# Decoder layer on one core: the first two batches of attention output products issued ahead of the third shifted scores

## The chip, the cores and the metric

The kernel runs on one core of a Trainium2 chip. The metric is the device time of one execution in microseconds; the time of a kernel is the median of several executions. The profile is of one more execution. Its engines are called PE (TensorE matmuls), PEld (TensorE weight loads), DVE (VectorE), ACT (ScalarE), POOL (GpSimd) and SP (SyncE, which here issues DMAs).

## What is computed

A pre-norm decoder layer over x of 128 batches x 128 tokens x 256 features, in float32, 16 heads of 16 features:

```
x = x + self_attention(layernorm(x))
x = x + cross_attention(layernorm(x), ctx, mask)
x = x + ffn(layernorm(x))          # 256 -> 1024 (ternary weights), gelu, layernorm, 1024 -> 256 (ternary weights)

attention: Q, K, V = projections with biases
           P = softmax(Q K^T / 4)          # in the cross attention, masked keys have the score 1e-9
           out = (P V) Wo^T + bo
```

Here the part that matters is one attention of a group of 4 batches, above all the last line, the output projection (P V) Wo^T: 4 batches of 128 x 256 by 256 x 256.

## The kernel before, in words

**Jobs and slots.** The 128 batches are worked on in 32 groups of 4. Each group has two attention jobs, self and cross, 64 jobs in all. The list `kinds` (in `attention`) orders them: six self jobs, then cross and self by turns, then six cross jobs. The jobs go through a pipeline that is written out as slots: in slot n, job n+4 is loaded, n+3 has its moments taken, n+2 is normalised (`s.norm`), n+1 is projected to Q and K (`s.proj`), n has its scores and row maxima made (`s.max`), n-1 has its exponentials and weighted values made (`s.exp`), and n-2 has its output products made (`s.out`). Jobs alternate between two sets of buffers and semaphores, the chains `even` and `odd`; inside a slot, `a` is the chain of jobs n, n+2 and n-2, and `b` that of n+1 and n-1. The attention part takes about the first 1780 us; the ffn part follows.

**Order.** Every engine has a program of its own for a slot, a fixed list of steps at the end of `act_slot`, `dve_slot`, `pe_slot`, `pool_slot` and `sp_slot`. An engine works its list strictly in that order and waits on semaphores inside the steps. There is no scheduler besides these lists.

**The steps of a slot on TensorE** (`pe_slot`, L1065). `scores(m)` (L1075), eight of them: Q K^T of job n for half the heads of a batch, into `score_bank` (matmuls of L1092, ahead of them in a cross job 4 mask matmuls of L1073). Each needs maximum m of VectorE, which reads the former scores out of this one buffer. `shifted(p)` (L1096), eight: the transposed scores of job n-1 with the row maxima already subtracted, into `exp_bank` (L1110, and in a cross job L1073). Each needs the exponential before it (ScalarE, L840), which empties the same buffer. `weighted(qd)` (L1114, matmuls L1125), four: P V into `out_bank`. `tile(n)` (L1149), four: the Q and K tiles of job n+1, into half `n % 2` of `product_bank`. `products(0, 1)` and `products(2, 3)` (L1160): the output products of job n-2, 2 batches each, 12 matmuls by `token_product` (L1156), also into `product_bank`. `values` (L1156 too): V of job n.

**What `products` waits for.** At batch 0 it waits for `a_lo`, the low half of the split attention output (GpSimd, `ahl`, L756), and, while there is a job to project, for all four `qk_lo` of this slot, since it writes over the Q/K tiles that VectorE still has to read:

```
if g == 0:
    pe.wait_ge(a.a_lo, 2 * s.out.k + 2)
    if s.proj:
        pe.wait_ge(b.qk_lo, 4 * s.proj.k + 4)
```

**The steps on VectorE** (`dve_slot`). `maximum(m)` (L936) reduces a block of scores to row maxima, `tile(n)` (L942) writes the low half of a Q/K tile (`qk_lo`), `outputs` (L970 to L985) turns and normalises P V, `turn_att` (L991) transposes it. The list of a slot reads:

```
outputs(a, s.out, 3); tile(0); turn_att(a, s.out, 1); maximum(0); tile(1); maximum(1)
maximum(2); tile(2); tile(3); maximum(3); outputs(b, s.exp, 0); maximum(4); maximum(5)
outputs(b, s.exp, 1); turn_att(b, s.exp, 0); maximum(6); outputs(b, s.exp, 2); maximum(7); ...
```

**The steps on ScalarE** (`act_slot`). `tile(n)` (L830) writes the high half of a Q/K tile, `exps(p)` (L840) makes the exponentials `prob` out of `exp_bank`, with `normalise`, `split_norm` (L864), `products_out` (L880) and `values_out` (L886) between them. GpSimd subtracts the high halves (L756) and adds residuals; SP issues the DMAs that stack Q and K by heads (L678) and transpose the normalised input (L688).

Of the kernel before, what the change touches and what calls it, by code (L numbers as in the profile page):

```python
# [588 lines left out]
def attention(nc, program, ins, sh, x1_dram, x2_dram, prep):  # L589
# [19 lines left out]
    with ExitStack() as stack:  # L609
# [56 lines left out]
        def stacked_by(count):  # L666

            return 16 * (STACK_DMAS * count + min(count, 2))
# [396 lines left out]
        def pe_slot(s, extra=None):  # L1065
# [3 lines left out]
            def add_mask(bank, mask):  # L1069
                for h in range(2):  # L1070
                    for r in range(2):
                        rows = slice(HALF * r, HALF * (r + 1))
                        pe.matmul(bank[:, r].rearrange("p (b s) -> p b s", b=G), sh.pick[rows, h], mask[rows, h].unsqueeze(1).broadcast_to([HALF, G, S]), start=(h == 0), stop=False, skip_group_check=True)  # L1073

            def scores(m):  # L1075
                if s.max is None:
                    return
                g, eight = divmod(m, 2)
                if m == 0:
                    pe.wait_ge(a.stacked, stacked_by(s.max.k + 1))  # L1080
                    if s.exp:
                        pe.wait_ge(b.mT_out, s.exp.k + 1)
                        if s.exp.cross:
                            pe.wait_ge(earg_ready, s.exp.g + 1)
                else:
                    pe.wait_ge(a.max_done, 8 * s.max.k + m)
                if s.max.cross:
                    add_mask(sbank, sh.maskB)
                for j in range(4):
                    for r in range(2):  # L1090
                        rows = slice(HALF * r, HALF * (r + 1))
                        last = pe.matmul(sbank[:, r, j * S:(j + 1) * S], a.stk[rows, s.max.k % 2, 0, j, eight, g * S:(g + 1) * S],  # L1092
                                         a.stk[rows, s.max.k % 2, 1, j, eight, g * S:(g + 1) * S], start=not s.max.cross, stop=True, skip_group_check=True)
                last.then_inc(a.s_mm, 1)

            def shifted(p):  # L1096
                if s.exp is None:
                    return
                if p == 0:
                    pe.wait_ge(b.m_in, 16 * (s.exp.k + 1))  # L1100
                if p:
                    pe.wait_ge(b.exp_done, 8 * s.exp.k + p)
                elif s.exp.cross:
                    pe.wait_ge(ue_ready, 2 * s.exp.g + 2)
                if s.exp.cross:
                    add_mask(ebank, sh.maskBT)
                for g in range(G):
                    for r in range(2):
                        rows = slice(HALF * r, HALF * (r + 1))
                        last = pe.matmul(ebank[:, r, g * S:(g + 1) * S], b.stk[rows, s.exp.k % 2, 1, p % 4, p // 4, g * S:(g + 1) * S],  # L1110
                                         b.stk[rows, s.exp.k % 2, 0, p % 4, p // 4, g * S:(g + 1) * S], start=not s.exp.cross, stop=True, skip_group_check=True)
                last.then_inc(b.st_mm, 1)
# [40 lines left out]
            def token_product(w, g, stationary):  # L1153
                for k, (part, wp) in enumerate(SPLITS):
                    for kt in range(KT):
                        last = pe.matmul(pbank[:, g // 2, g % 2 * D:(g % 2 + 1) * D], stationary(part, g, kt),  # L1156
                                         sh.WT[:, w, wp, kt, :], start=(k == 0 and kt == 0), stop=(k == 2 and kt == KT - 1))
                return last

            def products(*batches):  # L1160
                if s.out is None:
                    return
                for g in batches:
# [4 lines that stand above are left out]
                    last = token_product(s.out.wo, g, lambda part, g, kt: ahl[:, part, kt, g * S:(g + 1) * S])  # L1168
                if G - 1 in batches:
                    last.then_inc(a.op_mm, 1)  # L1170
# [51 lines left out]
            tile(3)  # L1222
            shifted(1)
            scores(2)
            shifted(2)
            if extra:
                extra(pe)
            weighted(0)
            scores(3)
            shifted(3)  # L1230
            products(0, 1)
            scores(4)
            shifted(4)
            weighted(1)
# [331 lines left out]
```

## Time and profile before

| | |
|---|---|
| median of 3 runs | 2356.61 us (2353.63 to 2359.61) |
| the profiled execution | 2356.74 us |
| its span | 2354.6 us |
| mean granted TensorE clock | 0.985 of full speed |
| busy share of the span | PE 92%, DVE 82%, ACT 68%, PEld 61%, POOL 44% |

The span is the time from the first to the last recorded instruction; the profiled execution's own time has 2.1 us around it. Rows of a timeline give start, duration, engine, line, operation, the tile written and the tiles read, the shape and how many instructions are merged; a bracket at the end gives the engine's idle time before the row and who ended it. The matmuls' ends are modelled: a group's duration contains the pipeline's depth, so the time that a group takes on TensorE is better read from its start to the start of the next one. Numbers in tile names are left out, and the two halves of the mask lines L1073 belong to `scores` or `shifted` by the bank that they write.

### The profile page before, as it was taken

Reading aid. Unit: us, or ns where it says so; the run is one execution under the profiler, and the core shown is the slowest. Engines: PE = TensorE matmul, PEld = TensorE weight load, DVE = VectorE, ACT = ScalarE, POOL = GpSimd, SP = SyncE. Lnnn points to the kernel's source line nnn. Section 1 sums busy time; section 2 is a strip of 40 time slices with the busy share of each in tenths; the row PEclk is TensorE's granted clock in tenths of the full one; section 3 lists DMA queues with packets and bytes.
Section 4 is the critical chain, followed back from the end, with each engine's and each line's share of the span. In section 5 each row is a group of like instructions: output and inputs, shape, how many; then the busy total and the mean of one; then the engine's idle time right before and its main releaser. Section 6 shows DMA issues by size and latency. Waiting matters only on the chain.

```text
span 2354.6 us, 70175 instructions
## 1 busy us (share of the span) xinstructions
PE 2173.1 (92%) x29001; PEld 1443.3 (61%) x29001; DVE 1933.5 (82%) x3903; ACT 1593.2 (68%) x2351; POOL 1047.5 (44%) x849
## 2 busy tenths in 40 slices
PE   4689999999999999999999999999967999999998
PEld 2455566556656665666566656665545777777776
DVE  6788888888888888888888888887745887887877
ACT  4376666676667666766666666665536778788786
POOL 3244444544443444344434444454224555555543
PEclk9799999999999999999999999999979999999999
DMA  6567666666766667676666676776322433333332
GB/s 169 141 160 170 141 152 150 157 154 159 154 156 146 145 154 158 158 153 160 147 156 145 153 157 160 154 177 143 91 77 55 98 89 80 105 83 87 100 81 63
DMA packets 477595, 314.14 MB, mean 133 GB/s; under 512 B 292368, under 2 KB 427408, under 8 KB 477328
## 3 DMA queue, kind: packets, MB, share of 16 engines
q1 hardware_dynamic: 474224, 309.95, 56.1%
q8 instruction: 204, 3.34, 0.6%
q10 hardware_dynamic: 3104, 0.34, 0.1%
q14 instruction: 63, 0.52, 0.1%
HBM read 72.69 MB, written 51.38 MB: 53 GB/s over the span
## 4 chain that ended last, share of the span: by engine, by line
PE 65%; DVE 17%; ACT 7%; issue 7%; DMA 2%; SPq 1%; POOL 1%; ACTq 0%; DVEq 0%; POOLq 0%
PE product_bank L1149 14%; PE ybk L1487 9%; PE hbk L1513 9%; PE out_bank L1125 7%; PE tbk L1501 5%; ACT prob L840 4%; PE product_bank L1156 4%; PE score_bank L1073 4%; DVE out_bank L970 4%; PE score_bank L1092 3%; DVE odd_mx L936 3%; PE exp_bank L1110 3%; PE exp_bank L1073 3%; PE exp_bank L1210 3%; DVE att L985 2%
## 5 line engine op out<-in xcount | busy, mean ns | idle before, releaser
L840 ACT ACTIVATE prob<-exp_bank 128x1024 f32<-128x1024 f32 x512 | 522.6, 1021 | 261.9 <-PE exp_bank L1110 253.9
L756 POOL TENSOR_TENSOR xs<-xn,xs 128x1024 f16<-128x1024 f32 x64 | 138.8, 2169 | 626.6 <-ACT xs L864 626.6
L936 DVE TENSOR_REDUCE even_mx<-score_bank 128x8 f32<-128x1024 f32 x256 | 310.6, 1213 | 92.8 <-PE score_bank L1092 92.8
L936 DVE TENSOR_REDUCE odd_mx<-score_bank 128x8 f32<-128x1024 f32 x256 | 310.4, 1212 | 79.8 <-PE score_bank L1092 79.8
L830 ACT ACTIVATE qk<-product_bank,bcol 128x512 f16<-128x512 f32 x256 | 175.7, 687 | 222.6 <-PE product_bank L1149 210.6
L1471 DVE SCALAR_TENSOR_TENSOR ghl<-tbk,lnwc,ghl 128x512 f16<-128x512 f32 x256 | 188.1, 735 | 99.9 <-ACT ghl L1402 99.8
L1513 PE MATMUL hbk<-wfcT,ffn_xhl 128*128 128x512 f16 x1024 | 262.2, 379 | 6.4 <-ACT hid L1408 3.6
L1487 PE MATMUL ybk<-wpT,ghl 128*128 128x256 f16 x2048 | 260.4, 273 | 0.8 <-DVE ffn_y L1456 0.7
L1487 PEld LDWEIGHTS ybk<-wpT,ghl 128*128 128x128 f16 x2048 | 197.8, 98 | 66.2 <-DVE ghl L1471 0.9
L1402 ACT ACTIVATE ghl<-tbk,lnwc 128x512 f16<-128x512 f32 x256 | 173.9, 680 | 67.8 <-PE tbk L1501 67.8
L942 DVE SCALAR_TENSOR_TENSOR qk<-product_bank,bcol,qk 128x512 f16<-128x512 f32 x256 | 184.3, 740 | 31.6 <-ACT qk L830 31.5
L970 DVE STREAM_TRANSPOSE out_bank<-out_bank 128x512 f32<-128x512 f32 x256 | 183.6, 717 | 24.8 <-PE out_bank L1125 24.2
L1073 PE MATMUL exp_bank<-maskBT,pick 64*128 64x512 bf16 x1024 | 156.0, 383 | 45.3 <-ACT prob L840 27.8
L1156 PE MATMUL product_bank<-WT,ahl 128*128 128x256 f16 x1536 | 192.0, 275 | 4.8 <-POOL ahl L756 4.8
L756 POOL TENSOR_TENSOR ahl<-attT,ahl 128x512 f16<-128x512 f32 x128 | 148.3, 1159 | 107.6 <-ACT ahl L845 107.6
L1149 PE MATMUL product_bank<-odd_xhl,WT 128*128 128x512 f16 x732 | 177.7, 387 | 11.2 <-DVE qk L942 6.9
L1432 DVE BATCH_NORM_STATS2 hstats<-hid 128x6 f32<-128x512 f32 x256 | 174.2, 681 | 14.3 <-ACT hid L1408 14.2
L1408 ACT ACTIVATE hid<-hbk 128x512 f32<-128x512 f32 x256 | 152.1, 595 | 49.1 <-PE hbk L1513 41.7
L1156 PEld LDWEIGHTS product_bank<-WT,ahl 128*128 128x128 f16 x1536 | 141.1, 98 | 33.9 <-POOL ahl L756 5.1
L1073 PE MATMUL score_bank<-maskB,pick 64*128 64x512 bf16 x1024 | 154.7, 381 | 6.5 <-DVE even_mx L936 5.7
L1501 PE MATMUL tbk<-ident,hid 128*128 128x128 f32 x1024 | 153.5, 273 | 0.7 <-ACT hid L1408 0.7
L1379 POOL TENSOR_TENSOR ffn_xs<-ffn_xn,ffn_xs 128x1024 f16<-128x1024 f32 x32 | 68.3, 2133 | 169.3 <-ACT ffn_xs L1419 169.3
(170 smaller groups left out, 4416.2 us busy)
## 6 DMA issues: line engine op xcount, KB each, us to landing
even_stk<-qk SPq DMA_DIRECT2D x384, 128.0 KB, 2.7
odd_stk<-qk SPq DMA_DIRECT2D x384, 128.0 KB, 2.8
x_scratch<-xn SPq DMA_DIRECT2D x64, 512.0 KB, 4.8
ctx_in<-in_ctx SPq DMA_DIRECT2D x32, 512.0 KB, 4.7
ffn_src<-x_scratch SPq DMA_DIRECT2D x32, 512.0 KB, 3.8
out<-ffn_y SPq DMA_DIRECT2D x32, 512.0 KB, 3.8
odd_src<-in_x SPq DMA_DIRECT2D x29, 512.0 KB, 5.5
even_src<-x_scratch SPq DMA_DIRECT2D x29, 512.0 KB, 5.8
```

The source lines that it names most:

```text
L756: nc.gpsimd.tensor_tensor(out, src, hi, ALU.subtract).then_inc(lo_ready, 1)
L840: act.activation(prob[:, p % 3], ebank[:, :, :], ACT.Exp, scale=EXP_SCALE).then_inc(b.exp_done, 1)
L936: dve.tensor_reduce(a.mx[:, g * H:(g + 1) * H].rearrange("p (r e j) -> p r e j", r=2, e=2)[:, :, eight], sbank[:, :, :].rearrange("p r (j ...
L942: dve.scalar_tensor_tensor(qk[:, 3 * (n // 2), n % 2], pbank[:, n % 2], sh.bcol[:, 2 * s.proj.which + n // 2, n % 2:n % 2 + 1], qk[:, 1 + ...
L970: dve.transpose(obank[:, 1], obank[:, 0]).then_inc(ch.o_turned, 1)
L1073: pe.matmul(bank[:, r].rearrange("p (b s) -> p b s", b=G), sh.pick[rows, h], mask[rows, h].unsqueeze(1).broadcast_to([HALF, G, S]), start= ...
L1149: last = pe.matmul(pbank[:, n % 2].rearrange("p (b s) -> p b s", b=G), sh.WT[:, (s.proj.wq, s.proj.wk)[n // 2], wp, kt, n % 2 * P:(n % 2 + ...
L1156: last = pe.matmul(pbank[:, g // 2, g % 2 * D:(g % 2 + 1) * D], stationary(part, g, kt), sh.WT[:, w, wp, kt, :], start=(k == 0 and kt == 0 ...
L1471: dve.scalar_tensor_tensor(ghl[:, LO, s], tbk[:, TURN_BANK[s]], sh.lnwc[:, s:s + 1], ghl[:, HI, s], ALU.mult, ALU.subtract).then_inc(glo_r ...
L1487: last = pe.matmul(ybk[:, b], ghl[:, part, t, b * S:(b + 1) * S], wpT[:, t], start=(t == 0 and part == HI and b % 2 == 0), stop=(t == FT - ...
L1501: last = pe.transpose(tbk[:, TURN_BANK[s], b * S:(b + 1) * S], hid[:, 1 - half, b, s * P:(s + 1) * P], sh.ident[:, :])
L1513: last = pe.matmul(hbk[:, s % 2], xhl[:, half, part, s // 2, kt], wfcT[:, kt, s % 2 * HF:(s % 2 + 1) * HF], start=(part == HI and kt == 0) ...
```

## The change

In TensorE's list of a slot, `products(0, 1)` moves from behind `shifted(3)` to the place between `scores(2)` and `shifted(2)`. Its waits move with it; the other engines' lists stay as they are.

```diff
@@ -1222,13 +1222,13 @@
             tile(3)
             shifted(1)
             scores(2)
+            products(0, 1)
             shifted(2)
             if extra:
                 extra(pe)
             weighted(0)
             scores(3)
             shifted(3)
-            products(0, 1)
             scores(4)
             shifted(4)
             weighted(1)
```

## Rows read from the trace of the kernel before

**Rows 1.** The page, busy time, share and instructions of each engine

```profile
PE 2173.1 (92%) x29001; PEld 1443.3 (61%) x29001; DVE 1933.5 (82%) x3903; ACT 1593.2 (68%) x2351; POOL 1047.5 (44%) x849
```

**Rows 2.** Waits of TensorE, 400 to 1700: us in total, times, longest

```profile
PE exp_bank L1073 <- ACT prob L840: 21.6, 26, 0.9
PE exp_bank L1110 <- ACT prob L840: 16.3, 23, 0.7
```

**Rows 3.** Timeline of TensorE, an odd slot

```profile
1021.60 0.61 PE L1073 MATMUL exp_bank<-maskBT,pick 64*128 64x512 bf16 x4 [0.90 <-ACT prob L840]
...
1022.36 1.08 PE L1125 MATMUL out_bank<-prob,even_vals 128*32 128x128 f32 x32
1023.38 0.40 PE L1092 MATMUL score_bank<-odd_stk 64*128 64x128 f16 x8
...
1024.36 1.49 PE L1156 MATMUL product_bank<-WT,ahl 128*128 128x256 f16 x12
1025.78 0.40 PE L1092 MATMUL score_bank<-odd_stk 64*128 64x128 f16 x8
...
1028.10 0.40 PE L1092 MATMUL score_bank<-odd_stk 64*128 64x128 f16 x8 [0.26 <-DVE odd_mx L936]
```

**Rows 4.** Timeline of VectorE, the same odd slot

```profile
1020.75 1.23 DVE L936 TENSOR_REDUCE odd_mx<-score_bank 128x8 f32<-128x1024 f32 x1 [1.16 <-PE score_bank L1092]
1021.89 1.40 DVE L942 SCALAR_TENSOR_TENSOR qk<-product_bank,bcol,qk 128x512 f16<-128x512 f32 x2
1023.82 1.22 DVE L936 TENSOR_REDUCE odd_mx<-score_bank 128x8 f32<-128x1024 f32 x1 [0.53 <-PE score_bank L1092]
...
1026.83 1.22 DVE L936 TENSOR_REDUCE odd_mx<-score_bank 128x8 f32<-128x1024 f32 x1
```

**Rows 5.** Timeline of ScalarE, the same odd slot

```profile
1020.52 1.02 ACT L840 ACTIVATE prob<-exp_bank 128x1024 f32<-128x1024 f32 x1
```

**Rows 6.** Timeline of GpSimd, the same odd slot

```profile
1017.17 1.16 POOL L756 TENSOR_TENSOR ahl<-attT,ahl 128x512 f16<-128x512 f32 x1 [2.67 <-ACT ahl L845]
```

**Rows 7.** Timeline of TensorE, the next slot, an even one

```profile
1047.01 0.40 PE L1110 MATMUL exp_bank<-odd_stk 64*128 64x128 f16 x8 [0.71 <-ACT prob L840]
...
1053.02 0.60 PE L1073 MATMUL score_bank<-maskB,pick 64*128 64x512 bf16 x4 [0.21 <-DVE even_mx L936]
```

**Rows 8.** Timeline of VectorE, the same even slot

```profile
1047.48 1.40 DVE L942 SCALAR_TENSOR_TENSOR qk<-product_bank,bcol,qk 128x512 f16<-128x512 f32 x2
```

**Rows 9.** Timeline of TensorE, a slot of self jobs, and one of cross jobs

```profile
142.48 0.40 PE L1110 MATMUL exp_bank<-even_stk 64*128 64x128 f16 x8 [1.14 <-ACT prob L840]
...
1658.07 0.61 PE L1073 MATMUL exp_bank<-maskBT,pick 64*128 64x512 bf16 x4 [0.47 <-ACT prob L840]
```

**Rows 10.** Timeline of VectorE, the same two slots

```profile
142.53 1.40 DVE L942 SCALAR_TENSOR_TENSOR qk<-product_bank,bcol,qk 128x512 f16<-128x512 f32 x2
...
1658.79 1.40 DVE L942 SCALAR_TENSOR_TENSOR qk<-product_bank,bcol,qk 128x512 f16<-128x512 f32 x2
```

**Rows 11.** Timeline of TensorE, around three idle stretches

```profile
91.95 0.40 PE L1092 MATMUL score_bank<-odd_stk 64*128 64x128 f16 x8 [2.83 <-DVE odd_mx L936]
...
92.68 1.75 PE L1125 MATMUL out_bank<-prob,even_vals 128*32 128x128 f32 x32
94.47 0.61 PE L1092 MATMUL score_bank<-odd_stk 64*128 64x128 f16 x8
...
1712.41 0.61 PE L1073 MATMUL exp_bank<-maskBT,pick 64*128 64x512 bf16 x4 [2.83 <-DVE ue L954]
...
1798.08 1.04 PE L1513 MATMUL hbk<-wfcT,ffn_xhl 128*128 128x512 f16 x4 [2.79 <-DMA ffn_xhl<-ffn_xs]
```

**Rows 12.** Stretches: length; busy by engine; granted clock, DMA share and GB/s last

```profile
93.00:99.50 6.50, 5.28 (x92) 3.90 (x84) 5.69 (x8) 3.63 (x4) 2.12 (x1) 0.50 0.25 48
1714.30:1717.60 3.30, 3.26 (x32) 1.61 (x29) 1.23 (x1) 1.10 (x2) 0.47 (x1) 0.50 0.00 0
1796.00:1804.00 8.00, 5.92 (x39) 3.99 (x40) 4.44 (x15) 4.58 (x10) 2.53 (x5) 1.00 0.45 104
```

## The prediction, as it was made

> **What bounds the kernel now.** I read the page first [rows 1]. TensorE is busy for 92% of the span, so whatever makes it stand still has a price. The table of waits then says what it waits for in the steady part [rows 2]: ScalarE's exponentials, some 0.7 to 0.9 us once in a slot (26 and 23 times), and little else. That hole lies ahead of a slot's shifted scores 3. (I count from one throughout: scores 3 is `scores(2)`.) The timeline of one slot whose exponentials belong to a cross attention (an odd slot) shows it: scores 3 end at about 1020.7, where maximum 3 starts on them [rows 4], then TensorE idles until 1021.60 [rows 3], because exponential 2 runs from 1020.52 to 1021.54 [rows 5] and only then frees the bank. VectorE in the same stretch [rows 4] is to be read as one queue: maximum 3 at 1020.75, behind it the low parts of Q/K tiles 3 and 4 from 1021.89, behind them maximum 4, which starts only when scores 4 have arrived (0.53 idle before it), then the transpose and the rest of `outputs(b, s.exp, 0)`, then maximum 5. Maximum 5 ends at 1028.05 and releases scores 6 on TensorE at 1028.10 (0.26 idle, named after VectorE) [rows 3, 4]. So from scores 4 to scores 6 a slot hangs on VectorE, with no slack: what delays scores 4 delays the slot.
>
> **The change, part by part.** Nothing is added or removed: the same 12 matmuls stand in another place, with their waits, and no DMA is issued with them; SP's and GpSimd's queues keep their order. What moves is the point at which TensorE must have (1) the low part of the attention output (`a_lo`) and (2) the fourth low part of this slot's Q/K tiles (`qk_lo`, four per job), since the products overwrite the bank that VectorE reads there.
>
> (1) costs nothing: GpSimd's `ahl` ends at 1017.17 + 1.16 = 1018.33 [rows 6], 2 us before the new place is reached.
>
> (2) is the heart of it. In the old place the wait had long been met: products at 1024.36 against VectorE's end at 1023.29 [rows 3, 4]. In the new place TensorE reaches it at about 1020.7, right after scores 3. But VectorE comes to tile 4 only after maximum 3, and maximum 3 needs just these scores. The stall can't be hidden: VectorE's 1.23 us of maximum and 1.40 us of two tiles, one behind the other, 2.6 us, in every slot. No other engine can shorten it: ScalarE's part of tile 4 is done before exponential 2 starts [rows 5].
>
> Odd slot: tiles end at 1021.89 + 1.40 = 1023.29; a hand-over of 0.05 as at 1028.05 to 1028.10; the products take 1.42 (1024.36 to 1025.78 [rows 3]); shifted scores 3 start at 1024.76 instead of 1021.60: **+3.16 us**. Behind them nothing changes up to scores 4 (shifted scores, weighted values, scores), so maximum 4 and all that follows come 3.16 later. What is gained back? The products leave a hole of 1.42 us between shifted scores 4 and scores 5. Scores 5 must wait for maximum 4, though, and maximum 5 stands behind VectorE's `outputs(b, s.exp, 0)`, which moves with maximum 4. The hole therefore becomes TensorE's idle time and gives nothing back. Queued behind the wait on TensorE are shifted scores 3, for which ScalarE's exponential 3 waits, and behind that its normalising and `split_norm`, then GpSimd's `xs` and SP's transposing DMA: all of them move by the same amount, so none becomes a new end.
>
> Even slot (masked scores, self exponentials): tiles end at 1047.48 + 1.40 = 1048.88 [rows 8]; with 0.05 and 1.42 the shifted scores 3 start at 1050.35 instead of 1047.01 [rows 7]: **+3.34**. Here too maximum 5 releases scores 6 at 1053.02 (0.21 idle) [rows 7]. After that TensorE itself is full, which carries the delay on.
>
> The first slots with both jobs self: 142.53 + 1.40 + 0.05 + 1.42 - 142.48 = **+2.92**. The last ones with both cross: 1658.79 + 1.40 + 1.47 - 1658.07 = **+3.59** [rows 9, 10].
>
> Count, from the schedule: a slot n has output products from n = 2 on, and Q/K tiles up to n = 62. Both-self: n = 2 to 5, 4 slots. Even pattern: n = 6, 8, ... 58, 27 slots. Odd pattern: n = 7, 9, ... 57, 26 slots. Both-cross: n = 59 to 62, 4 slots. Sum: 4 x 2.92 + 27 x 3.34 + 26 x 3.16 + 4 x 3.59 = 11.7 + 90.2 + 82.2 + 14.4 = **198.4 us**. Slot 63 has no Q/K tiles and so no wait (2): the products only push shifted scores 3 back, between 0 and 1.4; I take 1. Slot 64 has no scores and an idle stretch ahead of its shifted scores 3: taken as nothing, between -1.1 and 0.3 (a hole like the 1.1 of other slots of this kind against the 1.42). Both are inside rounding.
>
> **The clock.** The new stall puts an idle stretch of about 2.6 us (1.23 + 1.40) in each of 61 slots, where the steady part has none over 0.9 [rows 2]. The trace has three stretches of nearly that length that begin at full clock: 2.83 before 91.95 and 2.83 before 1712.41 were each followed by half clock, 2.79 before 1798.08 was not [rows 11, 12]. The granted clock, in rows that give it as a share of the full 2.4 GHz, stood at 0.50 (1.2 GHz) from 93.0 to 99.5 in one case and from 1714.3 to 1717.6 in the other, some 3.4 us [rows 12]. The price of one fall: 32 output matmuls at half clock take 1.79 (92.68 to the next at 94.47 [rows 11]) instead of 1.01 (1022.36 to 1023.37, the next group's start [rows 3]), a ratio of 1.77; 3.4 us at that rate do the work of 1.9 and lose 1.5. After the stall TensorE has over 3 us of unbroken work on the path to scores 4, so the loss is on the path. Bounds: 0 of 61 slots, and 61 x 1.5 = 92 us. Mine are a little shorter than the three stretches, of which two in three had it: I take half, 31 slots, **46 us**.
>
> A rule speaks for the lower end. The trace shows a fall of the clock after 2.83 us of idling. The Trainium skill, page "TensorE: Matmul & The Clock Gate", section "Why this matters for your kernels", tells one to avoid gaps over about 3 us between bursts of matmuls, which would leave this stall free of any fall; by it the sum would be 2556. The rows speak against it at 2.83 us, and since mine are shorter still, I keep it as a rival.
>
> **Sum.** The profiled execution took 2356.7 us (span 2354.6 and 2.1 around it), 0.1 over the median of the three runs, 2356.6. 2356.7 + 198.4 + 1 + 46 = **2602 us**, 10.4% slower.
>
> **The rivals.**
> (B) The stall as worked out, the clock never falls: 2356.7 + 199 = 2556. For it: the stretches are shorter than all three in the trace that I have. Against: two of these three had the fall.
> (C) The clock falls in nearly every slot, or stays low for twice as long in some: 2556 + 92 = 2648. For it: the long case of 6.5 us. Against: dense work follows the stall, as after 1714.3, where the clock came back after the short stretch.
> (D) The hole that the products leave is given back: scores 5 come 1.42 earlier against the rest, and if the second part of a slot hung on TensorE, not on VectorE, each slot would lose only 3.25 - 1.42 = 1.83: 61 x 1.83 = 112, 2468 without the clock's part. For it: even slots are full of TensorE work after 1053.02. Against: scores 6 are released by VectorE in both kinds [rows 3, 7].
> (E) Not slower. The products fill the hole of 0.7 to 0.9 us in which TensorE waits for exponential 2, and this hole is all that is felt. It decides at one point: VectorE's tiles must be done when scores 3 end, at 1020.7, 2.6 us before they are. Then 26 x 0.9 + 23 x 0.7, some 40 us, would go: 2317. Against: VectorE's order puts maximum 3, which needs these scores, first.
>
> **How the numbers follow.** Chances: forecast 0.50, B 0.30, C 0.10, D 0.07, E (or no difference) 0.03. The time is the forecast's, 2602. The range reaches from under B, with 0.3 us a slot for what I read too long, 2556 - 18 = 2538, to C, 2648. About 0.3% is what a measurement of this kernel can tell from no change: faster 0.02, within it 0.01, slower 0.97.
>
> **What would show it.** In the changed profile: a TensorE wait of about 2.6 us before `product_bank` L1156, named after VectorE's `qk` L942, some 61 times, 160 us in all; the wait of `exp_bank` for ScalarE's `prob` gone at this place; the time from the start of scores 4 to that of scores 6 as before; maximum 4 with more idle time ahead of it; slots of 28 to 30 us or, with the clock's fall, 1.5 more; the granted clock in the attention part under 1.00, near 31 x 3.4 / 1900 of it at half, which is 0.97. It is wrong if the wait is short (E), if slots grow by under 2 us (D), or if the steady part's clock stays at 1.00 (B).

## The result, and the profile after

| | before | changed |
|---|---|---|
| median, us | 2356.5 (4 runs, 2353.6 to 2359.6) | 2643.5 (4 runs, 2640.6 to 2646.1) |
| the profiled execution, us | 2356.74 | 2640.55 |
| its span, us | 2354.6 | 2638.8 |
| mean granted clock | 0.985 | 0.951 |

The ratio is 1.121 (95% interval 1.120 to 1.123): 12.1% slower, where 10.4% was forecast, 2643.5 against 2602, inside the range. The sign and most of the size were right, and 41 us were missing.

The page of the changed kernel, busy time by engine; it answers to [rows 1]:

```profile
PE 2261.6 (86%) x29001; PEld 1479.8 (56%) x29001; DVE 1933.4 (73%) x3903; ACT 1601.9 (61%) x2351; POOL 1047.7 (40%) x849
```

The instructions are the same in number. VectorE and GpSimd are busy for as long as before and ScalarE for 9 us more, only in a longer span. TensorE's busy time grew by 88 us for the same matmuls: some of them ran slower.

Waits of TensorE in the changed kernel, 140 to 2000; us in total, times, longest:

```profile
PE product_bank L1156 <- DVE qk L942: 163.7, 60, 2.7
PE score_bank L1073 <- DVE even_mx L936: 44.4, 58, 1.1
PE score_bank L1092 <- DVE odd_mx L936: 38.0, 56, 1.1
```

The first row is the new stall: 60 times 2.73 us, waiting for VectorE's Q/K tiles (one more, at 120.58, lies ahead of 140: 61 in all). The waits of [rows 2] for ScalarE no longer occur. The other two are the hole that the products left, as idle time ahead of scores 5 and 6: nothing was given back.

One even slot of the changed kernel. TensorE's timeline:

```profile
1024.00 0.39 PE L1092 MATMUL score_bank<-even_stk 64*128 64x128 f16 x8
1027.12 2.72 PE L1156 MATMUL product_bank<-WT,ahl 128*128 128x256 f16 x12 [2.73 <-DVE qk L942]
1029.77 0.61 PE L1110 MATMUL exp_bank<-odd_stk 64*128 64x128 f16 x8
1030.31 1.13 PE L1125 MATMUL out_bank<-prob,odd_vals 128*32 128x128 f32 x32
1031.37 0.61 PE L1073 MATMUL score_bank<-maskB,pick 64*128 64x512 bf16 x4
...
1033.53 0.61 PE L1073 MATMUL score_bank<-maskB,pick 64*128 64x512 bf16 x4 [1.10 <-DVE even_mx L936]
...
1036.05 0.61 PE L1073 MATMUL score_bank<-maskB,pick 64*128 64x512 bf16 x4 [0.46 <-DVE even_mx L936]
```

VectorE's timeline in the same slot:

```profile
1024.43 1.22 DVE L936 TENSOR_REDUCE even_mx<-score_bank 128x8 f32<-128x1024 f32 x1 [1.16 <-PE score_bank L1092]
1025.57 1.40 DVE L942 SCALAR_TENSOR_TENSOR qk<-product_bank,bcol,qk 128x512 f16<-128x512 f32 x2
1032.24 1.23 DVE L936 TENSOR_REDUCE even_mx<-score_bank 128x8 f32<-128x1024 f32 x1 [5.27 <-PE score_bank L1092]
...
1034.77 1.21 DVE L936 TENSOR_REDUCE even_mx<-score_bank 128x8 f32<-128x1024 f32 x1
```

The last matmuls of scores 3 are issued at 1024.00, maximum 3 follows at 1024.43, the two tiles at 1025.57, and the products when these are done. VectorE then stands idle for 5.27 us before maximum 4, where such a slot had some 0.3 before. From scores 4 to scores 6 the slot takes 4.68 us (1031.37 to 1036.05). An even slot of the kernel before took 4.67, from this row to the 1053.02 of [rows 7]:

```profile
1048.35 0.60 PE L1073 MATMUL score_bank<-maskB,pick 64*128 64x512 bf16 x4
```

What is new against the working of the prediction is the length of the products: from 1027.12 to 1029.77 they take 2.65 us, not the 1.42 of [rows 3].

Stretches of the changed kernel; length, then busy time of PE, PEld, DVE, ACT and POOL, then granted clock, DMA share, GB/s:

```profile
1023.00:1027.00 4.00, 1.39 (x22) 0.65 (x20) 2.81 (x4) 2.57 (x4) 0.28 (x1) 1.00 1.21 139
1027.00:1030.00 3.00, 2.88 (x18) 1.85 (x20) 0.00 (x0) 0.00 (x0) 0.00 (x0) 0.51 0.91 255
500.00:1500.00 1000.00, 849.94 (x12602) 534.35 (x12601) 728.12 (x1292) 581.70 (x780) 373.90 (x305) 0.94 0.56 129
```

The products run at half clock (1.2 GHz), right behind 2.73 us of idling. Over 1000 us of the steady part the clock is 0.94, where the same stretch before had 1.00:

```profile
500.00:1500.00 1000.00, 946.97 (x14958) 608.36 (x14958) 862.99 (x1535) 683.30 (x924) 443.69 (x362) 1.00 0.67 153
```

The trace's own record of the clock has 113 us at half there, in 31 falls of mostly 3.4 us, and 33 stalls lie in that stretch. Of all 61 stalls 55 have such a fall, which begins between 0.8 us before the products start and 1.0 us after; below, a "fall" is one that belongs to a stall in this way. The kernel before has a few falls of its own, at the very start and at the end of the attention part, and they are not counted. The forecast had 31.

The ffn part loses nothing: TensorE's waits in it are those of before within 0.3 us.

### The profile page after: what moved, and what is told of

Same layout as the page of the kernel before. It is cut to its first block, busy times and chain, and to the rows that moved or that the text cites. A ratio compares the mean times of both kernels' runs of the same rounds, so it can differ in the third digit from the quotient of the medians.

```text
span 2638.8 us, 70175 instructions
## 1 busy us (share of the span) xinstructions
PE 2261.6 (86%) x29001; PEld 1479.8 (56%) x29001; DVE 1933.4 (73%) x3903; ACT 1601.9 (61%) x2351; POOL 1047.7 (40%) x849
## 4 chain that ended last, share of the span: by engine, by line
PE 65%; DVE 23%; issue 6%; ACT 3%; DMA 1%; SPq 1%; POOL 1%; ACTq 0%; DVEq 0%; POOLq 0%
PE product_bank L1149 12%; PE product_bank L1156 9%; PE ybk L1487 8%; PE hbk L1513 8%; PE out_bank L1125 6%; DVE odd_mx L936 5%; PE tbk L1501 4%; PE score_bank L1073 4%; DVE out_bank L970 4%; PE score_bank L1092 4%; DVE qk L942 4%; DVE even_mx L936 3%; PE exp_bank L1110 3%; PE exp_bank L1073 2%; PE exp_bank L1210 2%
## 5 line engine op out<-in xcount | busy, mean ns | idle before, releaser
L1156 PE MATMUL product_bank<-WT,ahl 128*128 128x256 f16 x1536 | 258.8, 336 | 171.5 <-DVE qk L942 166.5
L1156 PEld LDWEIGHTS product_bank<-WT,ahl 128*128 128x128 f16 x1536 | 170.1, 117 | 231.3 <-issue 175.3
L1125 PE MATMUL out_bank<-prob,odd_vals 128*32 128x128 f32 x4096 | 141.8, 278 | 1.2 <-ACT prob L840 1.2
```

Of the source, the lines that this page charges most:

```text
L1125: last = pe.matmul(obank[VW * jq:VW * (jq + 1), 0, g * S:(g + 1) * S], b.vals[:, at:at + VW], prob[:, (2 * qd + jq // 2) % 3, jq % 2, g * ...
```

## The experiments

All were run beside the kernel before, whose median in these rounds was 2356.0 to 2356.5.

### 1 and 2. Matmuls that nobody reads, in the stall

```diff
+            def filler(count):
+                if s.out is None or s.proj is None or s.exp is None:
+                    return
+                pe.wait_ge(a.o_turned, 4 * s.out.k + 4)
+                for i in range(count):
+                    pe.matmul(obank[:, 0], ..., start=True, stop=True, skip_group_check=True)
...
             scores(2)
+            filler(10)
             products(0, 1)
```

> The changed kernel, with 10 matmuls of 128x512 that nobody reads put on TensorE into the new stall (into out_bank, written over by the next weighted values). They take about 10 x 0.225 = 2.25 us of the 2.7 us, so the wait for VectorE's tiles stays, with its end where it was, but TensorE isn't idle in it. Theory (the time beyond the stall is the clock, which falls in nearly every slot): the clock stays at 1.00 in the steady part, the wait named after VectorE's qk shrinks to some 0.4 us a slot, and the time falls from 2643 to 2356.5 + 199 = 2556. Rival (the extra 86 us are something else, such as a second wait behind the stall): the time stays at 2640, or rises.

Measured: 2560.5 us, ratio 1.086 (1.084 to 1.088).

> As the run with 10 idle-time matmuls, with 4 of them, 0.9 us, at the start of the stall: an idle stretch of 1.8 us stays. Theory: no stretch under 2 us was followed by a fall of the clock in the kernel before, so few or none here, and 2556 to 2575. If a stretch of 1.8 us is enough: about 2640, with some 55 low stretches. Rival (not the clock): 2640 with few low stretches.

Measured: 2558.3 us, ratio 1.086 (1.084 to 1.087). TensorE's timeline with 10 of them, then with 4:

```profile
1045.39 2.33 PE L1177 MATMUL out_bank<-WT 128*128 128x512 f16 x10
...
1048.19 1.47 PE L1156 MATMUL product_bank<-WT,ahl 128*128 128x256 f16 x12 [0.47 <-DVE qk L942]
```

```profile
1043.47 1.04 PE L1177 MATMUL out_bank<-WT 128*128 128x512 f16 x4
...
1046.27 1.47 PE L1156 MATMUL product_bank<-WT,ahl 128*128 128x256 f16 x12 [1.76 <-DVE qk L942]
```

and the stretch from 500 to 1500 in each:

```profile
500.00:1500.00 1000.00, 921.92 (x13570) 570.00 (x13569) 765.70 (x1365) 610.00 (x818) 397.22 (x324) 1.00 0.59 136
```

```profile
500.00:1500.00 1000.00, 877.90 (x13387) 550.24 (x13383) 765.73 (x1365) 609.86 (x818) 397.24 (x324) 1.00 0.59 136
```

The products wait just as long for VectorE, yet TensorE isn't idle for all of it, the clock stays at 1.00, the 12 products take 1.47 us again, and 83 to 85 us are gone by doing more work. What is left, 2558.3 - 2356.5 = 202, is the stall with the products in the path behind it, at full clock. The forecast had 199.4 for it. The fall of the clock cost (2643.5 - 2558.3) / 55 = 1.55 us each time, where 1.5 was forecast.

### 3. The wait alone

```diff
+            def await_tiles():
+                if s.out and s.proj:
+                    pe.wait_ge(b.qk_lo, 4 * s.proj.k + 4)
...
             scores(2)
+            await_tiles()
             shifted(2)
```

> The kernel before, with only the wait for the four qk_lo put ahead of shifted scores 3; the products stay in their old place. The stall is whole, the products' 1.42 us are not in the path. Theory: +1.74 an odd slot (1023.34 against 1021.60), +1.92 an even one, 1.50 and 2.17 in the 8 others, sum 112: 2468 without the clock; the idle stretch of 2.7 us is as long as in the changed kernel, so the clock falls here too in most slots, up to 1.4 us each: 2468 to 2553, likely near the upper end. Rival (it is the moved matmuls that cost, not the wait): near 2356.5 + 61 x 1.42 = 2443 or less, without a long stall.

Measured: 2538.2 us, ratio 1.077 (1.075 to 1.079). Waits of TensorE in this kernel, 140 to 2000:

```profile
PE exp_bank L1110 <- DVE qk L942: 79.2, 30, 2.6
PE exp_bank L1073 <- DVE qk L942: 79.2, 30, 2.6
```

60 stalls of 2.64 us, and a 61st ahead of 140. At 47 of them the clock falls; (2538.2 - 2468) / 47 = 1.49 us each, where 2468 is the time worked out for this kernel without the clock and not a measured one. So the wait, without any matmul moved, makes 182 of the 287 us.

### 4. The products left out of their old place

Half of the attention's output projection isn't computed here: in 61 slots the 12 matmuls of batches 0 and 1 are left out, and their waits stay.

```diff
                 for g in batches:
                     if g == 0:
                         ...
-                    last = token_product(s.out.wo, g, ...)
+                    if g > 1 or s.proj is None:
+                        last = token_product(s.out.wo, g, ...)
```

> The kernel before with the 12 matmuls of the first two batches of output products left out in 61 slots (so half of the attention output is not computed), their waits kept in the old place. Theory (from scores 4 on a slot hangs on VectorE, and the hole that the products leave gives nothing back): 2356, same as before within 5 us. Rival D (TensorE bounds this part, and a hole of 1.42 us is given back): 2356.5 - 61 x 1.42 = 2270.

Measured: 2358.2 us, ratio 1.0003 (0.999 to 1.001). TensorE's timeline, then VectorE's, in an odd slot:

```profile
1023.16 0.40 PE L1092 MATMUL score_bank<-odd_stk 64*128 64x128 f16 x8 [0.76 <-DVE odd_mx L936]
...
1026.08 0.40 PE L1092 MATMUL score_bank<-odd_stk 64*128 64x128 f16 x8 [0.65 <-DVE odd_mx L936]
```

```profile
1021.79 1.23 DVE L936 TENSOR_REDUCE odd_mx<-score_bank 128x8 f32<-128x1024 f32 x1 [0.53 <-PE score_bank L1092]
...
1024.81 1.21 DVE L936 TENSOR_REDUCE odd_mx<-score_bank 128x8 f32<-128x1024 f32 x1
```

732 matmuls, 61 x 1.42 = 87 us of work, are gone, and no time with them. The work turned into idle time ahead of scores 5 (0.76, none before) and scores 6 (0.65, where 0.26 was), and maximum 4 still has its 0.53. Rival D is out, and the products in their old place were free.

### 5 and 6. VectorE's tiles ahead of maximum 3

```diff
-            maximum(2)
-            more(2)
             tile(2)
             tile(3)
+            maximum(2)
+            more(2)
```

> The changed kernel, with VectorE's low parts of Q/K tiles 3 and 4 put ahead of its maximum 3. Theory (the stall is VectorE's order, 1.23 us of maximum and 0.7 of the tile before): tile 4 is done 0.8 us after ScalarE's part starts, at 1021.24 by the rows of the kernel before, so the wait shrinks from 2.7 to some 0.6 us; shifted scores 3 come 1.11 us later than in the kernel before in an odd slot, 1.29 in an even one: 2356.5 + 73 = 2430, with the clock at 1.00. Rival (the wait is not by this order, or the products cost at that place whatever the wait): a wait over 2 us, about 2560 to 2640.

Measured: 2432.5 us, ratio 1.033 (1.031 to 1.034).

> The kernel before with the same order on VectorE. Control for the run above: maximum 3 starts 0.4 us later and is still in time for scores 4, so 2356, same within 5 us. Rival (VectorE is so full that maximum 3's delay goes on): + 61 x 0.4 = 2381.

Measured: 2355.4 us, ratio 0.9998 (0.999 to 1.001). In the changed kernel with this order, TensorE's timeline of an odd slot, then VectorE's:

```profile
1009.10 1.47 PE L1156 MATMUL product_bank<-WT,ahl 128*128 128x256 f16 x12 [0.67 <-DVE qk L942]
```

```profile
1007.23 0.74 DVE L942 SCALAR_TENSOR_TENSOR qk<-product_bank,bcol,qk 128x512 f16<-128x512 f32 x1
1008.20 0.75 DVE L942 SCALAR_TENSOR_TENSOR qk<-product_bank,bcol,qk 128x512 f16<-128x512 f32 x1 [0.23 <-ACT qk L830]
```

Of the 2.73 us of stall, 2.06 are VectorE's order. The 0.67 that are left are the end of tile 4 itself, which VectorE starts 0.23 us late, waiting for ScalarE's part. The clock stays at 1.00 from 500 to 1500. 211 of the 287 us go, and the order by itself costs nothing. The place of the change is still worse than the old one by 76 us, because the hole ahead of shifted scores 3 (0.7 to 0.9 us) is shorter than stall and products together (0.67 + 1.4).

### 7. The products one step further back

```diff
             weighted(0)
+            products(0, 1)
             scores(3)
             shifted(3)
-            products(0, 1)
```

> The kernel before with the first two batches of products between weighted values 1 and scores 4. Theory (what counts is how late scores 4 come): no stall in an odd slot, so + the products' own 1.42; in an even one the wait lasts 0.6 us and shifts scores 4 by 2.0; 1.58 and 1.82 in the 8 others: sum 104, 2461, the clock stays at 1.00. Rival (the hole behind is given back): little above 2356.5 + 61 x 0.3 = 2375.

Measured: 2464.2 us, ratio 1.046 (1.045 to 1.048). TensorE's timeline of an odd and of an even slot:

```profile
1025.85 1.47 PE L1156 MATMUL product_bank<-WT,ahl 128*128 128x256 f16 x12
...
1052.89 1.47 PE L1156 MATMUL product_bank<-WT,ahl 128*128 128x256 f16 x12 [0.61 <-DVE qk L942]
```

Next to no stall, a full clock, and still 108 us: the products' 1.42 us ahead of scores 4 are paid in full, with the 0.61 us of an even slot (104 us were worked out from the two), and what opens behind scores 4 is not used.

### 8 and 9. Scores 4 earlier

```diff
-            weighted(0)
-            scores(3)
+            scores(3)
+            weighted(0)
```

> The kernel before with scores 4 ahead of weighted values 1 on TensorE, the other way round than the change. Theory (a slot hangs on when scores 4 arrive at VectorE): VectorE's 0.53 us (odd) and 0.34 us (even) of idling before maximum 4 go; TensorE's weighted values 2 then end last before scores 6 and leave 0.3 us an odd slot and 0.26 an even one: 2356.5 - 17 = 2340. Rival (the idle time before maximum 4 is not on the path, or the order makes another wait longer): 2356 or above.

Measured: 2357.0 us, ratio 1.0004 (0.9995 to 1.0013). A miss: 17 us expected, none found. TensorE's timeline, an odd slot and the even one behind it:

```profile
1022.50 0.61 PE L1073 MATMUL exp_bank<-maskBT,pick 64*128 64x512 bf16 x4 [0.90 <-ACT prob L840]
...
1028.67 0.40 PE L1092 MATMUL score_bank<-odd_stk 64*128 64x128 f16 x8
...
1047.58 0.40 PE L1110 MATMUL exp_bank<-odd_stk 64*128 64x128 f16 x8 [0.71 <-ACT prob L840]
1048.19 0.61 PE L1073 MATMUL score_bank<-maskB,pick 64*128 64x512 bf16 x4 [0.22 <-DVE even_mx L936]
...
1053.86 0.60 PE L1073 MATMUL score_bank<-maskB,pick 64*128 64x512 bf16 x4
```

From shifted scores 3 to scores 6 the odd slot takes 6.17 us instead of 6.50 (1021.60 to 1028.10, [rows 3]), as worked out. The even one takes 6.28 instead of 6.01 (1047.01 to 1053.02, [rows 7]): TensorE now comes to scores 4 before maximum 3 is done, idles 0.22, and all its work behind is late, scores 5 too. VectorE waits for those, 0.61 us before maximum 5, where it had no idle time before:

```profile
1052.58 1.22 DVE L936 TENSOR_REDUCE even_mx<-score_bank 128x8 f32<-128x1024 f32 x1 [0.61 <-PE score_bank L1092]
```

So in an even slot TensorE was hardly less the bound than VectorE: slack of 0.2 us, and this swap spent it. The same swap only where the exponentials are of a cross job (`if s.exp and s.exp.cross`):

> Scores 4 ahead of weighted values 1 only in slots whose exponentials are of a cross job (the odd ones, and the last ones). Theory from the run with the swap everywhere: an odd slot took 24.84 us instead of 25.17, an even one lost 0.3, because there TensorE waits 0.2 us for maximum 3 and brings scores 5 later than VectorE wants them. So 26 x 0.33 + 4 x 0.3 = 10 us less: 2346, 0.4% faster. Rival (the gain of an odd slot is lost in the next one in any case): 2356.

Measured in 7 runs: 2350.1 us against 2356.4, ratio 0.997 (0.996 to 0.998). 10 us less were expected and 6 are found. It is the one version here that beats the kernel before, by 0.3%.

### 10 and 11. How much idling it takes

> The changed kernel with 1 of the matmuls that nobody reads, 0.2 us, at the start of the stall: an idle stretch of 2.5 us stays. If the number of falls goes down with the stretch step by step, some 45 falls here, 2558 + 45 x 1.55 = 2628; if it is a matter of which length a slot has (the falls came in step with slots of 30.7 us), it stays near 55 falls and 2640. Rival (no fall below 2.6 us): 2558.

Measured: 2641.3 us, ratio 1.121 (1.119 to 1.122), 53 falls of the clock.

> The same with 2 of them, 0.45 us: an idle stretch of 2.25 us stays. Between 4 of them (1.76 us idle, no falls, 2558) and none (2.73 us, 55 falls, 2643). Step by step: some 30 falls, 2604; in step with the slots: near 50 falls, 2635; no fall below 2.5 us: 2558.

Measured: 2615.1 us, ratio 1.110 (1.108 to 1.112), 36 falls. All of it in one table, the changed kernel with the given number of matmuls in its stall:

| in the stall | idle stretch, us | falls at the 61 stalls | time, us | time over 2558.3, per fall |
|---|---|---|---|---|
| none | 2.73 | 55 | 2643.5 | 1.55 |
| 1 | 2.4 | 53 | 2641.3 | 1.57 |
| 2 | 2.2 | 36 | 2615.1 | 1.58 |
| 4 | 1.76 | 0 | 2558.3 | |
| 10 | 0.47 | 0 | 2560.5 | |

With 36, 53 and 55 falls the time follows their number at nearly 1.6 us each. Of the two readings given ahead of these runs neither fits both: the 53 of run 10 are near the 55 of the one by the slots' step, and the 36 of run 11 nearer to the 30 of the other than to 50.

## Why the prediction was right or wrong

**The wait is met too early, and VectorE's order sets it: right.** 61 waits of 2.73 us, 166.5 us in all, where 160 were given. Runs 5 and 6 show that it is this order: with the tiles first the wait is 0.67 us.

**The stall can't be absorbed, and delays scores 4: right.** 198.4 + 1 us were worked out; with the clock kept up, 202 are measured. One hand-over was taken too short: the products start 0.15 us after VectorE's tiles end (1025.57 + 1.40 = 1026.97 to 1027.12), not 0.05, which came from scores and not from products. Times 61 that would be 6 us, more than the 2.6 missing; what takes the rest back was not looked for.

**The hole gives nothing back (rival D): right**, by runs 4 and 7.

**"I take half, 31 slots, 46 us": wrong, and this is the step that failed.** The price of one fall was right (1.5 forecast, 1.55 measured), and that it would be on the path. The count was not: 55, not 31, so 85 us instead of 46. That makes up 39 of the 41 us missing. I had put the number by three single events of the trace before, two falls in three, and shaded it down because my stretches were shorter. Three events bear no such fine reading, and a steady loop isn't a draw of 61 lots: the falls came at even distances, in step with the slots (last section). The granted clock of the steady part, 0.94 where 0.97 was given as a sign, says the same. Rival C, nearly every slot, had 2648 and was the nearest, with a chance of 0.10. Why 55 and not another number stays open: runs 10 and 11 show that it depends on the length of the idle stretch, and not by what law. That 2602 still came near is owed to the stall, 199 of the 245 us forecast; the clock's part was off by nearly half.

The rule of the Trainium skill, page "TensorE: Matmul & The Clock Gate", section "Why this matters for your kernels", by which only gaps over about 3 us matter, gave 2556. The runs differ with it: gaps of 2.73 us cost the clock in 55 of 61 slots and gaps of 2.2 us in 36, and 1.76 us in none.

**A reading that was incomplete.** That the steady part has no idle stretch over 0.9 us holds for the two rows of [rows 2] only. Late in it TensorE stands still for 1.86 us before 1620.22 and 1.83 before 1651.90, and the clock stays up, as it does with 4 matmuls in the stall and 1.76 us left. It changes nothing in the sum.

**Rival E: out.** The waits for ScalarE at this place did go, as it says, but they were shorter than what took their place.

## What to carry to other kernels

Before moving work into another engine's hole, look up what its waits need at the new place and follow that engine's own order back: here the wait needed an instruction that stood behind one which needed the work just issued, so the gap was bound to open, and the 2.6 us of it can be worked out from four rows. Count then what an idle stretch of that length does to TensorE's clock, and do not take the share of rounds that have it from single events: here it was 55 of 61 at 2.73 us, 36 at 2.2 and none at 1.76. And if a stall can't be avoided, a few matmuls that nobody reads can pay: they gave back 85 of the 287 us here. They need a bank that is free at the time.

## What the runs showed that was not expected

The falls of the clock come in step with the slots. In the changed kernel 45 of the 54 distances from one fall to the next are 30.7 us, and a pair of slots takes 61.44 us (from tile 1 at 1016.09 to tile 1 at 1077.53), twice 30.72. Without the falls a pair would take 25.17 + 26.90 (the odd and the even slot of the kernel before, from tile 1 at 1012.83 to 1038.00 and to 1064.90) + 3.16 + 3.34 = 58.6. With one matmul in the stall it is the same distance again in most cases (41 of 52); with two, runs of falls 30.7 us apart alternate with gaps of 60 to 150 us without one. In run 3, whose slots are shorter, the distances go 27.3 and 30.7 by turns, with a gap of some 88 us now and then. Why these distances and no others was not tested.

4 matmuls in the stall did as well as 10 (2558.3 against 2560.5), though 1.76 us of idling were left.
